# Four graphs' distance and attention-logit products issued from 32 rows each, with new engine orders

## What is computed

```
# layer 1: the affinity that weighs the messages (s = 3 features a node)
s = x @ w_se.T + b_se
sq = jnp.sum(s * s, axis=-1)
dist = sq[:, :, None] + sq[:, None, :] - 2.0 * jnp.einsum('bnd,bmd->bnm', s, s)
A = jnp.exp(-dist) * mask
# layer 3: the logits of 4 heads, before the softmax
e = leaky_relu(e_i[..., :, None] + e_j[..., None, :])
e = where(adj > 0, e, -9e15)
```

## Time and profile before

| | us |
|---|---|
| median of 3 runs | 1428.95 (1428.47 to 1429.69) |
| the profiled execution, its own time | 1432.08 |
| span of its instructions | 1430.3 |
| mean granted TensorE clock over the span | 0.976 of full |

### The profile page before, as it was taken

How to read it: one execution, slowest core, us unless ns; L and a number is a source line. 1 busy time by engine, 2 the same in 40 slices (tenths; PEclk the granted TensorE clock), 3 DMA queues, 4 the chain that set the end, 5 groups by cost and what they waited for, 6 DMA issues and landing times.

```text
span 1430.3 us, 40514 instructions
## 1 busy us (share of the span) xinstructions
PE 1352.1 (95%) x13178; PEld 1075.1 (75%) x13267; DVE 1191.3 (83%) x3407; ACT 1188.4 (83%) x4353; POOL 663.1 (46%) x1014
## 2 busy tenths in 40 slices
PE   4799999999999999999999999999999999999964
PEld 3577788877778887777888777788877778887642
DVE  6568888888888888888888888888888888886763
ACT  3867888889888888998888899888889988887654
POOL 1133445554444555444455544445554444555532
PEclk7899999999999999999999999999999999999986
DMA  3100110011111001111100111111011111100000
GB/s 117 38 31 31 31 31 17 16 39 38 39 38 39 25 16 39 38 38 39 39 29 12 39 39 38 38 39 34 6 39 39 38 39 38 33 8 16 9 15 23
DMA packets 23825, 46.86 MB, mean 33 GB/s; under 512 B 2753, under 2 KB 2754, under 8 KB 23490
## 3 DMA queue, kind: packets, MB, share of 16 engines
q1 hardware_dynamic: 23618, 44.27, 9.8%
HBM read 35.88 MB, written 8.39 MB: 31 GB/s over the span
## 4 chain that ended last, share of the span: by engine, by line
PE 78%; DVE 10%; POOL 5%; issue 4%; ACT 3%; DVEq 0%; POOLq 0%; ACTq 0%
PE B L591 18%; PE B L689 14%; PE B L499 12%; PE B L537 5%; PE B L558 4%; DVE B L1353 4%; DVE x L1326 3%; POOL rstd L376 3%; PE B L808 2%; PE B L523 2%; PE B L788 2%; PE B L754 2%; PE B L581 2%; PE B L665 2%; PE B L683 2%
## 5 line engine op out<-in xcount | busy, mean ns | idle before, releaser
L995 ACT ACTIVATE e<-B,nm 128x128 f32<-128x128 f32 x1024 | 363.9, 385 | 12.5 <-DVE nm L1361 12.0
L499 PEld LDWEIGHTS B<-ident,e 128*128 128x128 f32 x1536 | 187.0, 144 | 104.3 <-issue 75.7
L499 PE MATMUL B<-ident,e 128*128 128x128 f32 x1536 | 230.0, 281 | 9.2 <-ACT e L1151 3.9
L995 ACT ACTIVATION_READ_ACCUMULATOR e<-B,nm 128x1 f32 x1024 | 231.9, 226 | 0.0
L1353 DVE SCALAR_TENSOR_TENSOR B<-an,rowb,mask 128x512 f32<-128x512 f32 x256 | 194.2, 794 | 19.0 <-ACT pT L1004 9.5
L1151 ACT ACTIVATE e<-l,nm 128x128 f32<-128x128 f32 x512 | 198.9, 400 | 10.0 <-DVE nm L1582 9.9
L1361 DVE TENSOR_REDUCE nm<-B 128x4 f32<-128x512 f32 x256 | 166.5, 683 | 35.0 <-PE B L537 34.8
L1004 ACT ACTIVATE pT<-B 128x512 f32<-128x512 f32 x256 | 157.9, 617 | 44.5 <-PE B L499 41.3
L373 POOL TENSOR_TENSOR veps<-meanv,eps 128x4 f32<-128x4 f32 x128 | 41.8, 326 | 328.9 <-DVE meanv L1320 328.8
L376 POOL TENSOR_TENSOR rstd<-veps,neghalf 128x4 f32<-128x4 f32 x128 | 139.7, 1092 | 10.0
L1582 DVE TENSOR_REDUCE nm<-l 128x4 f32<-128x512 f32 x128 | 87.0, 679 | 41.9 <-ACT l L1141 41.9
(11 more groups left out here) (201 smaller groups left out, 3471.1 us busy)
## 6 DMA issues: line engine op xcount, KB each, us to landing
xt<-in_x_t SPq DMA_DIRECT2D x32, 256.0 KB, 3.1
an<-in_adj_n SPq DMA_DIRECT2D x32, 256.0 KB, 2.7
xn<-in_x_n SPq DMA_DIRECT2D x32, 256.0 KB, 3.3
at<-in_adj_t SPq DMA_DIRECT2D x32, 256.0 KB, 3.2
out_x<-xo SPq DMA_DIRECT2D x32, 256.0 KB, 3.5
wm<-in_mats SPq DMA_DIRECT2D x1, 1088.0 KB, 9.4
wm<-in_mats SPq DMA_DIRECT2D x1, 832.0 KB, 7.1
wm<-in_mats SPq DMA_DIRECT2D x1, 320.0 KB, 3.0
```

What stands on the lines that cost most here:

```text
L499: last = mm(g(dst, b), g(src, b), ident[:, :], is_transpose=True, start=(b == 0), stop=True, skip_group_check=True)
L995: last = fn(g(e0[:, h % 2, :], b), g(bank, b), ACT.Exp, bias=nm0[:, h % 4, b:b + 1], accum_out=sum0[s % 2][:, b, head(h):head(h) + 1])
```

## The change

1. `sides` writes `lr` as one 128 x 128 tile in one instruction on all partitions (before: four on 9 partitions each). `distances` issues four products of 32 rows with 128 columns, into four banks, and `affinity` is four exponentials of 128 x 128.
2. `eim` is one 128 x 128 tile, made by one POOL instruction. `logits3` is one call for the four graphs: four mask products as before, one behind the other, then four products `eim` by `ejm` of 32 rows with 512 columns, each into the bank of its graph. The four banks are claimed together.
3. The orders of all five engines are new, with other banks and `users` lists; `STEPS` grows by 26 and all groups' offsets by some 25, which adds only steps with nothing live.

```diff
@@ sides (DVE), split_ej (POOL)
-                for b in range(GB):
-                    k = slice(32 * b, 32 * b + KS)
-                    v.scalar_tensor_tensor(out=lr[k, b * N:(b + 1) * N], in0=dd[k, :], scalar=sel[k, 0:1], in1=sqr[k, :],
-                                           op0=ALU.mult, op1=ALU.subtract)
+                v.scalar_tensor_tensor(out=lr[:, :], in0=dd[:, :], scalar=sel[:, 0:1], in1=sqr[:, :],
+                                       op0=ALU.mult, op1=ALU.subtract)
...
-                for b in range(GB):
-                    last = pool.tensor_scalar(eim[:, b, :], ejw[:, :], src_t[:, b:b + 1], src_i[:, b:b + 1], ALU.mult, ALU.add)
-                last.then_inc(q["ej_split"], 1)
+                pool.tensor_scalar(eim[:, :], ejw[:, :], src_t[:, :], src_i[:, :], ALU.mult, ALU.add)\
+                    .then_inc(q["ej_split"], 1)
@@ distances, logits3 (PE)
-                mm(bank[:, :], ll[:, :], lr[:, :], start=True, stop=True).then_inc(q["arg_ps"], 1)
+                for b in range(GB):
+                    k = slice(32 * b, 32 * b + 32)
+                    last = mm(banks[b][:, 0:N], ll[k, :], lr[k, :], start=True, stop=True)
+                last.then_inc(q["arg_ps"], 1)
...
                 pe.wait_ge(q["mask3_ready"], s + 1)
-                mm(bank[:, :], identb[:, :], g(mask3[s % 3], b).unsqueeze(1).broadcast_to([128, H3, N]),
-                   start=True, stop=False)
+                for b in range(GB):
+                    mm(banks[b][:, :], identb[:, :], g(mask3[s % 3], b).unsqueeze(1).broadcast_to([128, H3, N]),
+                       start=True, stop=False, skip_group_check=True)
                 pe.wait_ge(q["ej_split"], s + 1)
-                mm(bank[:, :], eim[:, b, :], ejm[:, :, :], start=False, stop=True).then_inc(q["e3_ps"], 1)
+                for b in range(GB):
+                    k = slice(32 * b, 32 * b + 32)
+                    last = mm(banks[b][:, :], eim[k, :], ejm[k, :, :], start=False, stop=True, skip_group_check=True)
+                last.then_inc(q["e3_ps"], GB)
@@ affinity (ACT)
-                fn(aT[:, :], bank[:, :], ACT.Exp).then_inc(q["em_ready"], 1)
+                for b in range(GB):
+                    last = fn(g(aT, b), banks[b][:, 0:N], ACT.Exp)
+                last.then_inc(q["em_ready"], 1)
@@ one line of DVE's new table, and one of SP's
+                seed_edges(t - 35, 7, B[4], (("x1T_ready", -2, 1, 1), ("oT_ready", -1, 1, 1),
+                    ("pT_ready", -1, 8, 8), ("r2_done", -4, 1, 1), ("em_ready", -3, 1, 1),
+                    ("hb_done", -4, 1, 1), ("exp_done", -1, 8, 8)))
...
+                store(t - 7)
```

More of the change, by code:

```diff
@@ L453, in step @@
             def step(t):
[L454 to L464, removed]
+                split_ej(t - 41)
+                fir_first(t - 39)
+                fir_second(t - 39)
+                rsqrt(1, t - 40)
+                mask_a(t - 39)
+                spread_sums(t - 37)
+                rsqrt(3, t - 42)
+                rsqrt(0, t - 38)
+                rsqrt(2, t - 40)
+                z_parts(t - 39)
+                z_times_x(t - 39)
             pool.wait_ge(q["const_set"], 2)
@@ L667, in message, with distances @@
                 last.then_inc(q["msg_ps"], 1)
[L669 removed]
+            def distances(s, banks, *users):
                 if not live(s):
                     return
[L672 removed]
+                for u in users:
+                    freed(pe, s, u)
                 pe.wait_ge(q["lr_done"], s + 1)
[L674 removed]
+                for b in range(GB):
+                    k = slice(32 * b, 32 * b + 32)
+                    last = mm(banks[b][:, 0:N], ll[k, :], lr[k, :], start=True, stop=True)
+                last.then_inc(q["arg_ps"], 1)
             def gather(s, bank, users):
@@ L1057, in message_relu, with affinity @@
                 fn(msg[:, :], msg[:, :], ACT.Relu).then_inc(q["msg_ready"], 1)
-            def affinity(s, bank):
+            def affinity(s, banks):
                 if not live(s):
@@ new lines, in step @@
+                keep_v(t - 36, B[1])
+                exps3(t - 41, 3)
+                keep_probs3(t - 41, 2, B[5])
+                keep_x3(t - 40, B[0])
+                keep_x1(t - 38, B[4])
+                keep_probs(t - 36, 1, B[6])
+                tanh_n(t - 39, B[1])
+                keep_ej(t - 40, B[0])
+                keep_d(t - 38, B[6])
+                exps(t - 36, 3, B[2])
+                keep_probs3(t - 41, 3, B[0])
+                conv_input(t - 38, B[6])
+                exps(t - 36, 4, B[3])
@@ new lines, in step @@
+                leaky(t - 40, 1, B[0])
+                exps3(t - 40, 0)
+                exp_edges(t - 39)
+                leaky(t - 40, 2, B[3])
+                affinity(t - 38, (B[4], B[7], B[0], B[1]))
+                exps3(t - 40, 1)
+                conv_relu(t - 38, B[6])
+                keep_probs3(t - 40, 0, B[3])
+                keep_q(t - 35, B[7])
+                leaky(t - 40, 3, B[5])
+                keep_gathered(t - 38, B[0])
+                keep_probs(t - 36, 6, B[3])
+                keep_h3(t - 40, B[2])
@@ new lines, in step @@
+                stats3(t - 40)
+                hidden_times_e(t - 38)
+                row_max3(t - 39, 1)
+                stats0(t - 36)
+                aggr3(t - 40)
+                row_max3(t - 39, 2)
+                edge_mask(t - 34)
+                row_scales(t - 38, (B[4], B[1]))
+                residual2(t - 38, (B[4], B[1]))
+                seed_edges(t - 34, 0, B[5], (("l3_done", -5, 4, 4), ("exp_done", -1, 8, 7),
+                    ("pT3_ready", -6, 4, 3), ("pT_ready", -1, 8, 1), ("exp_done", -1, 8, 1)))
@@ new lines, in step @@
+                seed_edges(t - 34, 3, B[2], (("h3_ready", -5, 1, 1), ("kh0_ready", 0, 1, 1),
+                    ("n3_done", -6, 1, 1), ("pT_ready", -1, 8, 4), ("exp_done", -1, 8, 4)))
+                invert_sums(t - 35)
+                aggr0(t - 36)
+                stats2(t - 38)
+                aggr2(t - 38)
+                row_max(t - 34, 0, B[5])
+                row_max(t - 34, 1, B[6])
+                row_max(t - 34, 2, B[0])
+                norm0(t - 36)
+                row_max(t - 34, 3, B[2])
```

478 lines of the change are left out of this document (218 added, 260 removed), and 3 rows, old and new, of the table last.

## The result

| | before | after |
|---|---|---|
| median, both kernels timed on one chip, 5 runs each | 1429.07 us | 1435.63 us (1433.97 to 1436.38) |
| ratio | 1 | 1.0043 [1.003, 1.0056] |
| profiled execution, its span | 1432.08, 1430.3 | 1435.63, 1433.6 |
| a step, mean of 15 in the middle of the span | 41.62 us | 41.66 us |
| `scores(s, 0)` to `scores(s, 1)`; on to the next `scores(s, 0)` | 20.31; 21.31 | 12.91; 28.75 |

The kernel is slower by 0.4%. The forecast was 1418, faster. The time lies inside the stated range, but on the other side of the kernel before; that it does so is luck, since the part of the range above 1430 was there for rival 1, whose sign, waits of PE over 0.4 us a step, is absent. The step, forecast at 41.3, is as long as before.

A forecast was written before the change was run, and what follows sets the result against it. PE was taken to bound the kernel; per step -0.75 us for both edits, +0.6 for the new order and waits of 0.1 instead of 0.3 gave 41.3, so 1428.95 - 11 = 1418 us, range 1407 to 1437.

The forecast's parts named there:

- rival 1: ACT chain from `scores(s, 0)` to `scores(s, 1)` outlasts PE's list, PE waits each step: 1431 to 1446, taken 1437; chance 0.19.
- What bounds the kernel: PE sets the time: a step is about 41.3 us of issue and 0.3 of waiting for `seed_edges`.
- Removed, 1.72: PE time leaving each step: distances product 0.86 us and four `eim` products together 0.86.
- Added, 0.97: PE time the packed pieces take per step: distances 0.53 us, four `eim` products 0.44, including changes in and out.
- The new order, +0.6: PE's reordered step: mode changes rise from six to eleven, without the new blocks, adding 0.6 us a step.
- Each change costs about 0.1: Every PE change between whole array, row tiles and column tiles was priced at about 0.1 us.
- The waits: The 0.3 us before `scores(s, 0)` goes; before `scores(s, 1)`, chain 12.7 against list 12.6, 0.1 is taken, not safely zero.
- The distances' 0.2 to spare: The distances' bank 4 waits for `hidden_bias`, which was to be about 0.2 us early.
- DVE and POOL, "off the path": DVE's 1.3 us saving was off the path; POOL's `split_ej`, 1.3 us shorter, ends over half a microsecond before it matters.
- ACT: The affinity's four exponentials instead of one add 0.2 us (bounds 0.1 to 0.9), with over 4 us free a step.
- The ends: PE's final wait of 4.71 us for `eim` gains 1 us; other fill and drain unpriced, 3 us either side.
- The sum: A step of 41.3 instead of 41.63, about 30 steps: -10 us; the end -1; so 1418 us.

The follow-up runs named there:

- before_split: Kernel before with one layer-3 transposition block moved between targets and the second half of the values, two mode changes more: 1443.19 us, ratio 1.0085.
- late_copy: Kernel after with the values' first half moved back to join the second, and ACT's copy `keep_probs3(t - 40, 1)` ahead of head 0's exponentials: 1432.00 us, ratio 1.0008.
- copy_early: Kernel after with only ACT's copy `keep_probs3(t - 40, 1)` moved ahead of head 0's exponentials: 1435.80 us, ratio 1.0039.
- run 3: Not a label: in "a run 3 us above its median" the words mean the profiled execution of the unchanged kernel before, 1432.08 us.
- copies_first: `late_copy` with two transpositions put behind tile blocks, ACT's head 1 copy directly behind head 0's, and x1T's copy ahead of x3T's: 1461.04 us, ratio 1.0219.

## Why the prediction was wrong, point by point

- **What bounds the kernel** was right: PE sets the time, and its 0.3 us of waiting went.
- **Removed, 1.72**, was right: whole again in the new order, the four `eim` products cost 0.86, and the distances 0.93, of which 0.07 by the wait ahead of them.
- **Added, 0.97.** From start to next the distances are 0.43 and the `eim` products 0.32, side by side, as forecast. But each exit into a float32 product adds 0.11 in the product behind it, and no term held that: with entries and exits the two cost 0.63 and 0.52, together 1.15. The net of both edits is -0.57, not the -0.75 of the sum.
- **The new order, +0.6: the step that failed.** The count, five changes more, was right. "Each change costs about 0.1" was not, and the 0.6 became 41.65 - 41.30 + 0.57 = 0.92. Before, the two exits went into a transposition and a bf16 mask, and the second hardly costs anything: mask and `eim` product behind the scores take 0.45 (827.02 to 827.47) instead of 0.43. In the new order four go into float32 products with weights (behind `scores(s, 0)`, the second half of the values, `eim`, distances) and two more than before into transpositions: 4 x 0.11 + 2 x 0.05 = 0.54, against the 0.50 by which the list exceeds 41.15 (0.18 of it in the term above, 0.32 in this one). The two that belong to the new blocks are in this sum. `before_split` (0.33 for two) and `late_copy` (0.26 for two) show what a pair costs. A price taken from pairs of operations was carried over to pairs of another kind. The Trainium skill ("TensorEngine Tiling (Array Packing)", Key Properties) says that a change of tiling mode drains the engine. It names no price; that the operation behind the change pays a part of it is what these rows add.
- **The waits.** 0.1 forecast, none found, but "not safely" was right to a tenth: rival 1's chain lies at 12.9 beside a list of 12.91. It did not decide after by itself, where `copy_early` gained nothing; the median of 1435.63 next to this rival's 1437 is no sign for it. It decided all four attempts to shorten the list alone. The distances' 0.2 to spare was 0.01.
- **DVE and POOL, "off the path"**, was wrong for the new order: without these savings it would be 0.95 and 1.2 us a step slower (1.18 - 0.23 and 1.54 - 0.34). As the sum took nothing for them, the forecast did not suffer; the reason did.
- **ACT.** The affinity's four exponentials cost what I gave them: 0.78 us (at 833.56) where one took 0.62, +0.16 for my +0.2; a step has 37.05 instead of 37.2.
- **The ends.** The wait of 4.71 for `eim` went, and the end didn't gain: in its place PE waits 4.70 for `hg` on DVE (at 1388.86) and 3.95 for a logits copy on ACT (at 1412.10). The fill takes 4.7 us less up to the eleventh `scores(s, 0)`, and from the last one to the end it takes 7.4 longer (173.8 instead of 166.4), in part only because the scores now stand elsewhere in the step. Span less the 21 steps between these two is 558.5, before 555.8: **+2.7**, and in `late_copy` it is 558.5. No run takes this apart; it stays open.
- **The sum.** Forecast -11 us; the spans differ by +3.3. Of these 14 us 21 x 0.37 = 8 lie in these steps, and 6 in fill and drain, for which the sum had nine of its thirty faster steps and the 1 at the end, -4, and the traces have +2.7. The medians differ by 6.6, not 3.3, because before was profiled in a run 3 us above its median; that other half is in no trace.

## What to carry to other kernels

Price a change of tiling mode by what stands on both sides of it, from rows with the same neighbours, and count exits by kind: a packing that saves 0.43 or 0.54 us of products, as here, gives back 0.2 of it if it stands alone between float32 products. When a list and a chain over another engine come out within a few tenths of each other, expect no gain from either alone, and test them together; follow the chain through every engine, since the engine that it is named after may only pass a wait on. An edit's relief of an engine "with slack" counts as soon as a new order is laid over it.

## What the hardware showed

- A float32 product behind a tile block costs 0.11 us more than in a row of its like, whether 512 columns (0.97 instead of 0.86) or eight of 128 (1.00 instead of 0.89); a transposition block 0.05. The entry costs 0.09. A float32 product behind a wait of 0.42 us, with no change of mode, cost 0.97 instead of 0.86 as well.
- Four bf16 products of 32 rows with 512 columns run side by side into four banks: 0.32 us from start to next, where four of 128 rows take 0.86.
- ACT was 89% busy in the middle of after, and a wait of 0.77 us put into its list in `copies_first` lengthened the step by 0.76.
